# Hybrid SSD mixer, one core: decay-score products on GpSimd, convolution silu and sums of squares on VectorE, and the exp of the decay rows made once for all groups

## The reference

```python
xBC = silu(conv4(xBC) + conv_b)             # causal convolution, 4 taps
L   = exp(segment_sum(A*dt))                # decay between two tokens of a chunk
Y_diag = einsum((C @ B.T) * L, x*dt)        # G * L in the kernel: the decay scores
Y_off  = einsum(C, states, exp(A_cumsum))   # exp(A_cumsum): the decay rows
y = (Y_diag + Y_off + D*x) * silu(gate)
y = y * rsqrt(mean(y*y over the group) + eps) * norm_w
out = y @ out_proj_w.T
```

## Time and profile before

| what | value |
|---|---|
| three runs | 2345.82, 2335.52 and 2347.23 us, median 2345.82 |
| the profiled execution | 2340.48 us, of which the span is 2338.4 us |
| PE busy | 2096.4 us (90%), granted TensorE clock 0.966 on average |
| DVE, ACT, POOL busy | 1585.1 us (68%), 1231.7 us (53%), 1152.2 us (49%) |
| loop over groups | 8 rounds of about 227 us |

### The profile page before, as it was taken

How to read it: one execution, slowest core, us unless ns; L and a number is a source line. 1 busy time by engine, 2 the same in 40 slices (tenths; PEclk the granted TensorE clock), 3 DMA queues, 4 the chain that set the end, 5 groups by cost and what they waited for, 6 DMA issues and landing times.

```text
span 2338.4 us, 39600 instructions
## 1 busy us (share of the span) xinstructions
PE 2096.4 (90%) x11776; PEld 1731.7 (74%) x11776; DVE 1585.1 (68%) x2766; ACT 1231.7 (53%) x2680; POOL 1152.2 (49%) x987
## 2 busy tenths in 40 slices
PE   3889998989999989999998899899989888989897
PEld 2678777877777777777787778777777767767775
DVE  5797489739973996498659956984698463167314
ACT  2676367627762775377437744864476323522341
POOL 0377247814781578157716661765277414330332
PEclk7999999999999999999999999999999999999999
DMA  2343034203421342044113412331243027941894
GB/s 69 123 127 90 19 100 131 73 29 104 128 63 37 111 130 64 24 118 134 48 49 109 128 37 70 104 113 37 71 115 101 19 100 279 404 140 44 283 392 150
DMA packets 143765, 261.22 MB, mean 112 GB/s; under 512 B 19521, under 2 KB 35905, under 8 KB 143553
## 3 DMA queue, kind: packets, MB, share of 16 engines
q1 hardware_dynamic: 134848, 231.35, 31.2%
q0 software_dynamic: 7520, 24.65, 3.3%
q10 hardware_dynamic: 1184, 2.62, 0.3%
HBM read 233.38 MB, written 25.17 MB: 111 GB/s over the span
## 4 chain that ended last, share of the span: by engine, by line
PE 40%; issue 25%; POOL 21%; DVE 11%; ACT 1%; another core or an unknown queue 1%; POOLq 0%; DMA 0%; DVEq 0%; SPq 0%; ACTq 0%
PE bank L1475 25%; PE bank L1758 5%; POOL gt L681 5%; POOL Y L692 5%; POOL cv L699 4%; POOL Y L675 3%; PE bank L1608 3%; POOL wl L659 2%; PE bank L1770 2%; PE bank L1622 1%; DVE mem L1226 1%; POOL mem L650 1%; DVE Y L1184 1%; PE bank L1745 1%; DVE mem L1152 1%
## 5 line engine op out<-in xcount | busy, mean ns | idle before, releaser
L1475 PE MATMUL bank<-xh,wh 128*128 128x512 f32 x1288 | 522.2, 405 | 17.2 <-POOL wl L659 10.3
L1475 PE MATMUL bank<-xh,wl 128*128 128x512 f32 x1288 | 504.1, 391 | 0.0
L1475 PE MATMUL bank<-xl,wh 128*128 128x512 f32 x1288 | 503.5, 391 | 0.0
L659 POOL TENSOR_TENSOR wl<-raw,wh 128x512 fp32r<-128x512 f32 x144 | 183.9, 1282 | 511.1 <-ACT wh L857 510.5
L1184 DVE SCALAR_TENSOR_TENSOR Y<-bank,cpar,Y 128x511 f32<-128x511 f32 (+2 forms) x384 | 287.0, 747 | 21.3 <-ACT Y L874 11.1
L1475 PE MATMUL bank<-wh,ah 128*128 128x512 f32 x576 | 241.7, 420 | 65.7 <-DVE wl L1139 24.3
L1475 PEld LDWEIGHTS bank<-xh,wh 128*128 128x128 f32 x1288 | 243.2, 189 | 65.8 <-issue 12.2
L1475 PEld LDWEIGHTS bank<-xh,wl 128*128 128x128 f32 x1288 | 242.6, 188 | 52.6
L1475 PEld LDWEIGHTS bank<-xl,wh 128*128 128x128 f32 x1288 | 243.5, 189 | 45.1 <-issue 0.5
L1249 DVE TENSOR_TENSOR al<-Y,ah 128x512 fp32r<-128x512 f32 x128 | 108.8, 856 | 201.0 <-ACT ah L937 201.0
L650 POOL TENSOR_TENSOR mem<-mem,hpt 128x384 f32<-128x384 f32 x128 | 106.7, 834 | 275.9 <-DVE mem L1152 259.3
(11 more groups left out here) (211 smaller groups left out, 4228.7 us busy)
## 6 DMA issues: line engine op xcount, KB each, us to landing
mem<-c_rows SPq DMA_DIRECT2D x176, 256.0 KB, 3.6
mem<-wffn_d SPq DMA_DIRECT2D x62, 512.0 KB
E<-c_rows SPq DMA_DIRECT2D x256, 96.0 KB, 2.8
raw<-wconv_d SPq DMA_DIRECT2D x80, 256.0 KB, 2.8
cv<-c_rows SPq DMA_DIRECT2D x80, 256.0 KB, 3.6
raw<-wgate_d SPq DMA_DIRECT2D x64, 256.0 KB, 2.7
raw<-wout_d SPq DMA_DIRECT2D x64, 256.0 KB, 2.6
slots_y<-quad SPq DMA_DIRECT2D x62, 256.0 KB
```

The lines of the kernel that those rows point to most:

```text
L659: inc(pool.tensor_tensor(wl[:, W_SLOT[p], :], raw[:, R_SLOT[p], :], wh[:, W_SLOT[p], :], ALU.subtract), w_lo)
L1475: got = mm(out, l, r, start=first and n == 0, stop=last and n == 2)
```

## The change

The products G * L (two instructions per unit, steps 10 to 25) go from DVE to POOL, where they stand behind L650 and ahead of the low part of a weight. The silu of the later 11 convolutions goes from POOL, where it was two instructions, to DVE, where it is one, as for the first 9. The sum of squares goes from POOL to DVE, behind the gate. The exp of the decay rows is made once in the preparation (one activation of 128x1024, and a second DRAM tensor `e_rows`), and the E tiles are loaded from it, so that ACT's L847 falls away, and DVE instead of ACT waits for the DMA.

```diff
@@ gpsimd, step k @@
                             .to_broadcast([P, CH - 1, 2, HD]), ALU.mult), xd_ok)
+                    u = k - A_ - 1
+                    if 0 <= u < UNITS:
+                        pair, b = unit(u)
+                        for h in range(2):
+                            n = 2 * u + h
+                            now(pool, decay_ok, i, n + 1)
+                            if n == 0:
+                                now(pool, g_ok, i, 2)
+                            inc(pool.tensor_tensor(L[n % LR], L[n % LR],
+                                    G[:, b * CH:(b + 1) * CH, :].rearrange("p c i -> p (c i)"),
+                                    ALU.mult), lg_ok)
...
-                    kc = k - 1
-                    if EARLY <= kc < NCONV:
-                        now(pool, conv_th, i, kc + 1)
-                        dst = piece(*conv_unit(kc))
-                        inc(pool.tensor_tensor(gt[:, kc % 2, :], dst, gt[:, kc % 2, :], ALU.mult), conv_vt)
-                        now(pool, conv_vt, i, kc - EARLY + 1)
-                        inc(pool.tensor_tensor(dst, dst, gt[:, kc % 2, :], ALU.add), conv_late)
...
-                    n = k - 3 - NCONV
-                    if BATCH <= n < NGATE:
-                        now(pool, sq_ok, i, n + 1)
-                        if n >= 2 * BATCH:
-                            now(pool, ss_add, i, n - 2 * BATCH + 1)
-                        inc(pool.tensor_tensor(acc[:, n % 2, :], acc[:, n % 2, :], sq[:, n % 2, :], ALU.add), ss_add)
@@ scalar, preparation @@
             act.dma_start(c_rows.rearrange("g h n -> (g h) n"), c_hm).then_inc(scr_rows, 16)
+            n = step(nc.scalar.activation(v_hm, c_hm, ACT.Exp))
+            act.wait_ge(act_step, n)
+            act.dma_start(e_rows.rearrange("g h n -> (g h) n"), v_hm).then_inc(scr_rows, 16)
@@ scalar, step k @@
-                        e_arrived(act, i, u)
-                        inc(nc.scalar.activation(E[:, u % ER, :], E[:, u % ER, :], ACT.Exp), e_ok)
@@ sync, scales_in @@
-                        sp.dma_start(E[h * HD:(h + 1) * HD, u % ER, :], c_rows[i, a:a + 1, b * SEQ + P:(b + 1) * SEQ]
+                        sp.dma_start(E[h * HD:(h + 1) * HD, u % ER, :], e_rows[i, a:a + 1, b * SEQ + P:(b + 1) * SEQ]
@@ vector, step k @@
                     kc = k - 1
-                    if 0 <= kc < EARLY:
+                    if 0 <= kc < NCONV:
                         tile, b = conv_unit(kc)
                         dst = piece(tile, b)
                         now(dve, conv_th, i, kc + 1)
-                        inc(STT(dst, gt[:, kc % 2, :], 1.0, dst, ALU.add, ALU.mult), conv_early)
+                        inc(STT(dst, gt[:, kc % 2, :], 1.0, dst, ALU.add, ALU.mult), conv_ok)
...
                     if 0 <= u < UNITS:
                         now(dve, off_mm, i, u + 1)
-                        now(dve, e_ok, i, u + 1)
+                        e_arrived(dve, i, u)
...
-                    u = k - A_ - 1
-                    if 0 <= u < UNITS:
-                        pair, b = unit(u)
-                        for h in range(2):
-                            n = 2 * u + h
-                            now(dve, decay_ok, i, n + 1)
-                            if n == 0:
-                                now(dve, g_ok, i, 2)
-                            inc(TTn(L[n % LR], L[n % LR],
-                                    G[:, b * CH:(b + 1) * CH, :].rearrange("p c i -> p (c i)"),
-                                    ALU.mult), lg_ok)
...
                         inc(last, gate_ok)
+                    n = k - 3 - NCONV
+                    if BATCH <= n < NGATE:
+                        now(dve, sq_ok, i, n + 1)
+                        if n >= 2 * BATCH:
+                            now(dve, ss_add, i, n - 2 * BATCH + 1)
+                        inc(TTn(acc[:, n % 2, :], acc[:, n % 2, :], sq[:, n % 2, :], ALU.add), ss_add)
```

More of the change, by code:

```diff
@@ L170, in hybrid_layer @@
         c_rows = nc.dram_tensor("c_rows", (GROUPS, GH, TOK), f32, kind="Internal").ap()
+        e_rows = nc.dram_tensor("e_rows", (GROUPS, GH, TOK), f32, kind="Internal").ap()
         xn_dram = nc.dram_tensor("xn_dram", (TOK, HID), f32, kind="Internal").ap()
@@ L207, in hybrid_layer @@
         conv_th = counted("conv_th", NCONV)
-        EARLY = 9
-        conv_early = counted("conv_early", EARLY)
-        conv_vt = counted("conv_vt", NCONV - EARLY)
-        conv_late = counted("conv_late", NCONV - EARLY)
+        conv_ok = counted("conv_ok", NCONV)
         tr_mm = counted("tr_mm", 2 + 2 + UNITS)
@@ L216, in hybrid_layer @@
         dcol_ok = counted("dcol_ok", 2)
-        e_ok = counted("e_ok", UNITS)
         fall_ok = counted("fall_ok", 2 * UNITS)
@@ L378, in conv_done @@
         def conv_done(eng, i, n):
-            if n <= EARLY:
-                now(eng, conv_early, i, n)
-            else:
-                now(eng, conv_late, i, n - EARLY)
+            now(eng, conv_ok, i, n)
         T_B, T_G, T_X, A_, B_, C_, D_ = 4, 6, 8, 9, 10, 11, 11
@@ L419, in hybrid_layer @@
         PH_PREP, PH_MIXER = 1, 2
-        PREP = dict(dt=13, scan=16, tokc=18, diff=20, tables=20, decay=9, cend=11)
+        PREP = dict(dt=13, scan=16, tokc=18, diff=20, tables=20, decay=10, cend=12)
         FFN_ORDER = [("gu", 0, 0), ("gu", 1, 0), ("gu", 0, 1), ("dn", None, 0), ("gu", 1, 1), ("dn", None, 1)]
@@ L501, in _ @@
                             hp_in, 16)
-                        sp.wait_ge(scr_rows, 16)
+                        sp.wait_ge(scr_rows, 32)
                         sp.wait_ge(phase, 4 * PH_PREP)
@@ L591, in _ @@
         def _(pool):
-            credit(pool, (w_lo, g_ok, conv_vt, conv_late, xd_ok, y_ok, y_gated, ss_add, f_lo))
+            credit(pool, (w_lo, g_ok, lg_ok, xd_ok, y_ok, y_gated, f_lo))
             steps = [0]
@@ L755, in _ @@
         def _(act):
-            credit(act, (w_hi, tap0, conv_th, tr_act, g_act, fall_ok, decay_ok, e_ok, gate_th, sq_ok,
+            credit(act, (w_hi, tap0, conv_th, tr_act, g_act, fall_ok, decay_ok, gate_th, sq_ok,
                          nrm_sd, y_hi, f_hi, f_th, a_hi))
@@ L865, in _ @@
                         if k == 4:
-                            act.wait_ge(scr_rows, 16)
+                            act.wait_ge(scr_rows, 32)
                             act.wait_ge(scr_heads, 16)
@@ L1022, in _ @@
         def _(dve):
-            credit(dve, (wo_lo, taps, conv_early, lg_ok, xs_ok, s_step, s_ok, off_ok, ydiag_ok, gate_ok, dcol_ok,
+            credit(dve, (wo_lo, ss_add, taps, conv_ok, xs_ok, s_step, s_ok, off_ok, ydiag_ok, gate_ok, dcol_ok,
                          nrm_ok, y_lo, res_ok, f_hg, f_h, a_lo, dn_acc))
```

## The result

The changed kernel took 2354.61 us, median of 7 runs (2349.68 to 2360.94), beside 2345.82 us for the kernel before in 7 runs (2335.52 to 2349.85). The ratio is 1.0048, with a 95% interval of 1.0031 to 1.0066: half a percent slower. The measured time lies inside the predicted 2336 to 2358 us, 7 us above the 2348 that was written down; the terms it was added up from were not so good, as the stretches show.

The account below looks back on a forecast made before the run. DVE was taken to bound steps 11 to 19, PE most of the rest. Terms of -0.6, -1.0, +0.2 and +2.2 made +0.8 us per group, +6.4 in all, 2346.9, written as 2348 us; range 2336 to 2358, chance 0.42.

Parts of the forecast that it names:

- The first term: Step 10: the product pair leaves DVE (1.2 us), the silu comes (0.6), a gain of 0.6 us per group.
- rival 3: POOL bounds steps 15 to 23 through late L rows, 7.4 us a step: 2367 us, range 2359 to 2378, chance 0.24.
- The exclusion of DVE and POOL: A DVE instruction with two SBUF inputs and a POOL instruction never overlap; silu 1.2 to 1.8 us instead of 0.68.
- Steps 11 to 19: DVE relief gains 2.0 us per group, late L rows cost some 1.6; a gain of 1.0 was taken.
- Steps 20 to 26: 1.1 us back in step 20, but 7.4 us a step in steps 21 to 23: +0.2 us per group.
- Steps 27 to 36: Weight, gate and sum of squares become serial, 3.13 us a step against PE's 2.75: +2.2 us per group.
- over seven steps DVE falls 2.7 us behind: From step 27, DVE's serial 3.13 us a step against PE's 2.75 delays the last weight part PE waits for.
- step 37 and on: The last sum of squares comes behind L1249 while PE works on the second output tile: no effect.
- Rival 1: PE's waits for L1152 ahead of the transposes simply go: 2273 us, or 2291 with the tail; 2268 to 2300, chance 0.12.
- Rival 2: Silu mostly goes ahead of POOL, steps 11 to 19 last 6.46 to 6.6 us each: 2317 us, 2305 to 2328, chance 0.16.
- Rival 4: The exp made once is worth something by itself on ACT; put within 2 us of nothing, no chance given.

Follow-up runs that it names:

- experiments 4 and 5: Parts done alone on the kernel before: exp made once 0.9978, sums of squares on DVE 0.9923; products back on DVE in the changed kernel 0.9926.
- Experiment 6: Silu moved behind DVE's two products with a bank operand: 2328.17 us from the changed kernel, 2259.23 us with L rows also issued ahead of weights and E rows.
- a_rows_top: Changed kernel with SP issuing a step's L rows ahead of both its weight piece and its E rows: 2272.8 us, ratio 0.9694.
- a_rows_first: Changed kernel with SP issuing a step's L rows ahead of its E rows only: 2294.71 us, ratio 0.9798.
- experiment 5: Single parts done or undone: sums of squares on DVE in before 2326.57 us; in the changed kernel, sums on POOL 2379.7, silu on POOL 2407.57, products on DVE 2324.2.
- a_prod_dve: Changed kernel with the two products G * L back on DVE: 2324.2 us, ratio 0.9926.
- b_ss_dve: Kernel before with only the sums of squares moved from POOL to DVE: 2326.57 us, ratio 0.9923.

## Why the prediction came out right, and where its steps did not

**Right in the sum, by terms that offset each other.** Predicted per group were -0.6, -1.0, +0.2 and +2.2, in all +0.8 us. The four stretches moved by -0.60, +0.93, +1.33 and -0.94 (up to the next group's step 9), and the period by +0.79. Seven periods are 5.5 of the 9.2 us by which the spans differ, and the last group's steps 9 to 26 another 1.2; before the first group the changed kernel is 1.9 us ahead, and behind the last one's step 27 it loses 4.3. The first term is right; the two in the middle are too low by 1.9 and 1.1 us, and the last too high by 3.1. The sum owes its precision to chance. The parts of experiments 4 and 5 say it in another way: exp -0.2%, sums of squares -0.8%, products +1.2%. Two of the prediction's own sums don't come out as written, without weight for its number: three steps of 0.4 less 1.1 are +0.1 and not +0.2, and rival 3 speaks of a tail at 3.4 us but adds 1.0; with 3.4 its terms make 5.7 us per group and 2386 us, outside the 2359 to 2378 given to it.

**The exclusion of DVE and POOL: right.** The silu took 1.52 us in steps 11 to 19 (1.2 to 1.8 said), and steps 11 to 14 took 6.92, 6.63, 6.91 and 6.63 us (7.0 and 6.7 in turn said). Of the 160 silus of the changed kernel 40 found POOL idle, at 0.68 to 0.69 us; the 120 that found it running took 1.28 on average, up to 1.84, and the 28 of them that took under 0.76 us began within 0.21 us of the end of POOL's instruction. L1202, with a bank as one operand, took 0.73 to 0.75 with POOL running (81 times) and 0.73 to 0.74 with it idle (47). Experiment 6 shows it as a cause. The Trainium skill, in "SBUF — State Buffer", section "SBUF: two separate sides", gives the ports that the two engines share to one instruction at a time, where DVE's has two SBUF inputs; with that rule the trace agrees. The Trainium skill, in "Perfetto Trace Analysis", section "Optimizing Scalar/DVE Operations", warns that moving work between these two may not help. The products bear that out as they were placed, with their 1.2%. But what they cost went through the late rows and not only through the exclusion: in a_rows_top, with the products on POOL all the same, the whole change gains 3.1%.

**Steps 11 to 19: the step that failed.** The prediction put the late rows at some 1.6 us at most, against a gain of 2.0 from DVE, and took a gain of 1.0. The chain POOL's sum, SP, L rows, L892 was named and its links were right, but I let it close only beyond a sum at 6.2 us. It closed in steps 15 and 18 of nearly every group. I had also left out its second entry, SP's wait for the weight pieces, which stands ahead of both kinds of rows. That is the part that cost 22 us, the difference of a_rows_first and a_rows_top. Measured by a_rows_top, late rows cost 65.19 - 60.70 = 4.5 us of these nine steps. Not all of that need be waiting: the granted clock is at its lower level for 5.1 us of these steps per group in the changed kernel and never in a_rows_top, and no run separates the two.

**Steps 20 to 26: the mechanism right, the size off.** The chain was said to give 7.4 us in each of steps 21 to 23. It gave 8.6, 6.6 and 8.7 in the third group, 7.9 on average over the groups, and 8.8 in step 18; late rows cost 43.33 - 38.98 = 4.4 us here by the same run. This was rival 3's mechanism, and for these two stretches rival 3 was the better account, with four long steps instead of nine at 7.4 us. Its own sign did not come, though: POOL was to be never idle from step 15 to 26, and it was busy for 81 to 85% of that time in each group. It was the chain and not POOL's load that set the long steps, and rival 3 too had no term for what the sums of squares give back.

**Steps 27 to 36: the round right, its cost mis-sized, and the gain behind it missing.** The DVE round of weight, gate and sum of squares did become serial, as said. In the changed kernel it looks like this:

```profile
683.12 0.67 DVE L1214 SCALAR_TENSOR_TENSOR gt<-gt,bank 128x512 f32<-128x512 f32 x1
683.72 0.68 DVE L1222 TENSOR_TENSOR cv<-cv,sq 128x512 f32<-128x512 f32 x1
683.87 1.68 POOL L690 TENSOR_TENSOR Y<-Y,gt 128x512 f32<-128x512 f32 x1 [1.23 <-DVE gt L1214]
684.32 1.78 DVE L1132 SCALAR_TENSOR_TENSOR wl<-raw,gpar,wh 128x512 fp32r<-128x512 f32 x1
...
697.87 0.50 PE L1462 MATMUL bank<-wh,ah 128*128 128x512 f32 x1 [2.64 <-DVE wl L1132]
```

It takes 2.90 us (683.12 to 686.02), not 3.13. PE's wait is 2.64, not 5, and the stretch 30.1 us instead of 32.7. The third group and the seventh are the two best of the eight: in the other six the stretch takes 30.9 to 31.0 us and PE waits 2.8, and the average is 30.75, against 30.51 in before. So the term of +2.2 us measured +0.2. The step that failed is "over seven steps DVE falls 2.7 us behind": against PE's 2.75 it is 1.05 us, and in before POOL, full for 27.44 of 27.50 us, had been as far behind, with its round of 2.96. The other failed term is that of step 37 and on, put at nothing: from the second half of step 36 to the next step 9 the changed kernel takes 80.1 us instead of 81.2, a gain of 1.1 that goes with the granted clock, as told in experiment 5.

**The rivals.** Rival 1 fell: PE's waits for the transposes are 89.6 us. Rival 2 fell too: steps didn't go to 6.5. Rival 4 was off by little: the exp alone gives 5 us, not under 2. Its greater worth, that DVE needs the E rows later than ACT did and the issue order becomes free, was not in the prediction.

**What stays open.** No run has the L rows first and the products on DVE together with the rest of the change, so it isn't shown that the products are better on POOL even then; that a_rows_top is faster than a_prod_dve (0.9694 against 0.9926) mixes both edits. It isn't shown either what keeps the granted clock at its lower level for longer in some rounds behind step 36 than in others. And the stretch behind the eighth group's step 27, which no edit touches but for its first steps, lasts 528 to 539 us in these kernels in no order that I can tie to the edits (531.1 before, 535.4 changed). Differences of up to 5 us between single kernels mean little for that reason.

## What to carry to other kernels

When work is moved onto an engine, ask first whose release it delays, and what is written behind that release in the queue of the DMA issuer: here a wait for a buffer, 1.7 us on average and up to 5.0, held back a transfer that didn't need it, and putting that transfer ahead of this wait and of the one for the weights made the same change 3% faster than before instead of half a percent slower. Look at every wait ahead of it in that queue: freeing the first alone moved the stop to the second, and gained 7 us. And where two engines exclude each other, place an instruction of one where the other is idle before moving it across.

## What the hardware showed that I had not expected

PE idle for the same 2.64 us ahead of step 36's second half was followed by a lower clock in one kernel and not in the other. The changed kernel, then b_ss_dve:

```profile
697.90:711.80 13.90, 11.73 (x52) 9.75 (x53) 4.81 (x9) 4.37 (x7) 0.00 (x0) 0.88 0.24 76
```

```profile
695.40:707.70 12.30, 10.12 (x53) 8.64 (x53) 4.82 (x9) 4.37 (x7) 0.00 (x0) 1.00 0.25 86
```

The same work took 1.6 us longer, part of it at the lower of the clock's two levels (1.2 GHz). In b_ss_dve PE idles for 2.64 us there in every group, and of the seven rounds the first, fourth and seventh have the long form behind it and the others the short one. In before, with 3.03 us idle, all seven have the long form. What decides it no run here isolates.
